# A transformer decoder in float32: its first part with three units in flight instead of two, and the loads and the gated network behind it rearranged

## The chip, the cores and the metric

One program runs on one core of a Trainium2 chip. The metric is device time in microseconds (us) of one execution. TensorE (PE; its weight loads PEld), VectorE (DVE), ScalarE (ACT) and GpSimd (POOL) run their own instruction streams in program order and wait for each other on semaphores; SyncE (SP) issues the large transfers. TensorE's results go to PSUM, eight banks of 128 x 512 float32.

## The reference

Input x is 32 sequences of 64 tokens, 128 wide, with a context of the same shape and coordinates of 3. Four layers follow; each adds to x the result of a self attention, a cross attention and a feed-forward network, each on a layer-normed x. Cut to the part that the change touches:

```python
x = x + L0_attn(ln(x), ...)          # 16 "heads" of 8, mixed over features
x = x + L0_xattn(ln(x), ctx, ...)    # softmax(q k^T / sqrt(8)) v, 16 heads
x = x + L0_ffn(ln(x), ...)           # silu(gate) * up, 384 hidden, dequantized weights
x = x + L1_attn(ln(x), ...)          # 16 heads, ternary weights
x = x + L1_xattn(ln(x), ctx, ...)    # scores of the heads mixed by a 16 x 16 matrix P
x = x + L1_ffn(ln(x), ...)           # every activation rounded to a 16 bit grid whose step
                                     # is max(abs(whole tensor)) / 32767
x = x + L2_...(x) ; x = x + L3_...(x)
```

L1_ffn needs the maximum over all 2048 tokens before it can round, four times in a row. L3's cross attention rotates queries and keys by sines and cosines of the coordinates.

## The kernel before, in words

Tokens are on partitions in 16 tiles of 128; two tiles (four sequences) make a **unit**, so there are eight. After a prologue the work has three parts with a barrier (`all_done`) between them.

**Part one** takes each unit through L0_attn, L0_xattn, L0_ffn, L1_attn, L1_xattn and the norm of L1_ffn. Two streams run side by side, each with four PSUM banks (`PS0`, `PS1`) and one arena `AR` in SBUF; four rounds make the eight units. Each engine's program is written as Python generators, one for each stream, which yield between steps; `take_turns` deals the steps out by a hand-written table `TURNS_A`, so the order on each engine is fixed in the code. On PE a third chain, `tensor_fill`, stands in the table: each step is one 128 x 128 matmul of the identity whose result nobody reads (L493). The string `FILL_A` has 471 of them.

In L0_xattn and L1_attn the 16 heads are held in four strips of 32 partitions. L745 multiplies the scores, strip r into bank r; DVE takes the maxima (L591); PE turns them over (L610); L616 computes the scores again, transposed, and L619 subtracts the maxima in the same banks; ACT takes the exponentials (L603); L641 weighs the values. In L1_xattn, L732 writes the mixed scores of a quarter of the heads into bank r, r = 0 to 3, and DVE takes the maximum (L541) and subtracts (L544).

**Part two** is L1_ffn over all tokens at once (`tensor_l1_ffn`, `scalar_l1_ffn`, `vector_l1_ffn`), in four chunks of 512 tokens. Each of its rounding steps ends in `tensor_scales` and `vector_scales`: PE turns the 128 partial maxima into a row (L1202), DVE takes its maximum, PE spreads it over partitions (L1205). Between them PE does work for part three: products of L2 weights (L1184, which need `WC`, the weights of part three), sums of gate weights (L1235, from `stat`, loaded in two halves), transposes of the sines and cosines (`tensor_angles`, L1241) and their spreading over partitions (`tensor_rotation`, L1249, a matmul of 8 rows by 512 columns), which ACT copies to `ROT` (L1305). `tensor_idle` (L1229) multiplies an identity by 512 columns into a bank that nobody reads. L1298 is the network's last product.

**Part three** is L2 and L3 in two streams.

Of the kernel before, what the change touches and what calls it, by code (L numbers as in the profile page):

```python
# [37 lines left out]
def constants():  # L38
# [22 lines left out]
    rows = np.arange(8)[:, None]  # L61
    c["sin_sel"] = np.pad(np.where(rows == d % 4, np.where(d < 4, -1.0, 1.0), 0.0), ((0, P - 8), (0, 0)))
    c["cos_sel"] = np.pad((rows - 4 == d % 4) * 1.0, ((0, P - 8), (0, 0)))
# [114 lines left out]
def decoder(nc, x, ctx_in, coords, const_d, aw_d, raw_d, intw_d, cw_d, stat_d, fd_d, out, known):  # L178
    es = ExitStack()
    with es:  # L180
# [29 lines left out]
        stream_sems = [[sem(f"{e}_stream{s}") for e in engine_names] for s in range(NS)]  # L210
        streams = [Stream(stream_sems[s], s, known) for s in range(NS)]
        SC = sb("SC", [P, NS, 640])
        for s, st in enumerate(streams):
# [12 lines left out]
            st.sc = SC[:, s, :]  # L226
        asides = [Stream(stream_sems[s], s, known, twin=st) for s, st in enumerate(streams)]
# [53 lines left out]
        S.dma_start(WC[:, :], cw_d).then_inc(wc_there, 16)  # L281

        every = [main, *streams]

        def begin(st, part, i):

            st.round = f"{part}{i}"
            tile, col = i * (NS * TS) + st.s * TS, i * (NS * ST) + st.s * ST
            st.x, st.cols = X[:, tile:tile + TS, :], slice(col, col + ST)
            st.ct = CT[:, st.cols]  # L290
# [89 lines left out]
        def pool_prologue():  # L380
            v, g = main.dve, main.pool
            for st in streams:
# [133 lines left out]
        def tensor_values(st, k, src, weight, bank):  # L516
            w4_ = weight.rearrange("p (r g n) -> p r g n", r=GR, g=2)
            for q in range(SQ):
                for g in range(2):
                    m = T.matmul(st.ps[64 * g:64 * g + 64, bank, q * SEQ:(q + 1) * SEQ],  # L520
# [3 lines left out]
        def scalar_values(st, k, bank):  # L524
            A.wait_ge(*st.pe.at(f"{k}.values"))
            for g in range(2):
                rows = slice(64 * g, 64 * g + 64)
                A.copy(st.vo[rows, :, g, :, 0:HD],
                       st.ps[rows, bank, 0:SQ * SEQ].rearrange("p (n h d) -> p n h d", h=2, d=HD)).then_inc(
                    *st.act.up(f"{k}.values{g}"))  # L530

        def vector_softmax(st, k, width, E):
            v = st.dve
            for r in range(GR):
                n = 512 // width
                sc3 = st.ps[:, r, :].rearrange("p (a k) -> p a k", k=width)
                er = E[:, 512 * r:512 * r + 512]
                mx = st.sc[:, 64 + 8 * r:64 + 8 * r + n]
                yield
                V.wait_ge(*st.pe.at(f"{k}.scores{r}"))  # L540
                V.tensor_reduce(mx, sc3, AX, ALU.max).then_inc(*v.up())  # L541
                yield
                V.wait_ge(*v.now())
                V.tensor_tensor(er.rearrange("p (a k) -> p a k", k=width), sc3, bc(mx, 2, width),  # L544
                                ALU.subtract).then_inc(*v.up(f"{k}.below{r}"))
                yield

        def scalar_softmax(st, k, parts, scale):

            def kept(u, r):
                A.wait_ge(*u.pe.at(f"{k}.turned{r}"))
                A.copy(parts(u)[1][:, 512 * r:512 * r + 512], u.ps[:, r, :]).then_inc(*u.act.up(f"{k}.turned{r}"))

            E = parts(st)[0]
            for r in range(GR):
                er = E[:, 512 * r:512 * r + 512]
                yield
                A.wait_ge(*st.dve.at(f"{k}.below{r}"))  # L560
                A.activation(er, er, ACT.Exp, scale=scale).then_inc(*st.act.up(f"{k}.exps{r}"))
                yield
                if r:
                    kept(st, r - 1)
                    yield
            kept(st, GR - 1)
            yield

        def tensor_softmax(st, k, parts, weigh, lag):


            E = parts(st)[0]
            for r in range(GR):
                yield
                T.wait_ge(*st.act.at(f"{k}.exps{r}"))
                for n in range(4):
                    m = T.transpose(st.ps[:, r, n * P:(n + 1) * P], E[:, (4 * r + n) * P:(4 * r + n + 1) * P], ident)
                m.then_inc(*st.pe.up(f"{k}.turned{r}"))
                yield
                if r >= lag:  # L580
                    weigh(st, r - lag)
                    yield
            for r in range(GR - lag, GR):
                weigh(st, r)
            yield
# [63 lines left out]
        def tensor_attention_weigh(k):  # L649
            def weigh(st, r):  # L650
                T.wait_ge(*st.act.at(f"{k}.values1"))
                T.wait_ge(*st.act.at(f"{k}.turned{r}"))
                tensor_weigh(st, k, attention_parts(st)[1], r)
            return weigh

# [25 lines left out]
        def tensor_project(st, k, weight):  # L681
            for j in range(TS):
                m = T.matmul(st.ps[:, 3, j * P:(j + 1) * P], lhsT=st.ot[:, j * P:(j + 1) * P], rhs=weight,
# [4 lines left out]
        def vector_project(st, k, scale_o, res):  # L688
            yield
            V.wait_ge(*st.pe.at(f"{k}.out"))  # L690
            V.scalar_tensor_tensor(st.x[:, :, :], st.ps[:, 3, 0:ST].rearrange("p (j d) -> p j d", d=P), scale_o, res,
# [6 lines left out]
        def tensor_attention(st, k, w, src, mix=False, rope=False):  # L698
            ps, ar = st.ps, st.ar
            E, AT = ar[:, 4096:6144], ar[:, 6144:8192]  # L700

            def keys():
                for n, wn in enumerate(("Wk", "Wkp") if rope else ("Wk",)):
# [3 lines left out]
                tensor_values(st, k, src, w(f"{k}_Wv"), 1)  # L707

# [3 lines left out]
            if own:  # L712
                yield from keys()
                yield
            for n, wn in enumerate(("Wq", "Wqp") if rope else ("Wq",)):
                m = T.matmul(ps[:, 0, n * ST:(n + 1) * ST], lhsT=w(f"{k}_{wn}"), rhs=st.xt[:, :], start=True, stop=True)
            m.then_inc(*st.pe.up(f"{k}.qk"))
            yield
            if mix:
                qp = ar[:, 0:16 * ST].rearrange("p (q g t) -> p q g t", q=SQ, g=H)  # L720
                kf = AT[:, ST:2 * ST]
                T.wait_ge(*st.act.at(f"{k}.values1"))
                for r in range(GR):
                    yield
                    T.wait_ge(*st.dve.at(f"{k}.qp{(3, 4, 11, 12)[r]}"))
                    if r in (1, 3):
                        T.wait_ge(*st.act.at(f"{k}.qp{(0, 7, 0, 15)[r]}"))
                    for q in range(SQ):
                        for g in (2 * r, 2 * r + 1):
                            o = q * P + (g % 2) * SEQ  # L730
                            for h in range(2):
                                m = T.matmul(ps[64 * h:64 * h + 64, r, o:o + SEQ], lhsT=qp[:, q, 2 * g + h, :],  # L732
                                             rhs=kf[:, q * SEQ:(q + 1) * SEQ], start=True, stop=True)
# [2015 lines left out]
```

## Time and profile before

| | |
|---|---|
| device time, median of 3 runs | 1527.18 us (1524.0 to 1532.17) |
| the profiled execution | 1525.39 us, of which its span 1524.1 us |
| part one, from 29.0 to 463.6 us of the span | 434.6 us |
| part two, to 563.1 us | 99.5 us |
| part three, to the end | 960.9 us |
| PE busy over the span | 92% |
| DVE, ACT, POOL busy | 69%, 41%, 8% |

Every fp32 matmul stands in the trace as two records, every transpose as one. Busy time of PE includes the matmuls whose results nobody reads.

### The profile page before, as it was taken

Reading aid. Unit: us, or ns where it says so; the run is one execution under the profiler, and the core shown is the slowest. Engines: PE = TensorE matmul, PEld = TensorE weight load, DVE = VectorE, ACT = ScalarE, POOL = GpSimd, SP = SyncE. Lnnn points to the kernel's source line nnn. Section 1 sums busy time; section 2 is a strip of 40 time slices with the busy share of each in tenths; the row PEclk is TensorE's granted clock in tenths of the full one; section 3 lists DMA queues with packets and bytes.
Section 4 is the critical chain, followed back from the end, with each engine's and each line's share of the span. In section 5 each row is a group of like instructions: output and inputs, shape, how many; then the busy total and the mean of one; then the engine's idle time right before and its main releaser. Section 6 shows DMA issues by size and latency. Waiting matters only on the chain.

```text
span 1524.1 us, 43988 instructions
## 1 busy us (share of the span) xinstructions
PE 1403.8 (92%) x19476; PEld 1227.7 (81%) x19476; DVE 1054.4 (69%) x2951; ACT 624.9 (41%) x1253; POOL 128.7 (8%) x267
## 2 busy tenths in 40 slices
PE   4999999999998689999988999988999988999986
PEld 3888888888884358989777998977998977998876
DVE  5758668578576958656677766678776677865666
ACT  4334344353364844532432543433543332542322
POOL 2111111111111000010000000000000000000000
PEclk9999999999999779999998999999999999999998
DMA  8000000000001110000000000000000000000001
GB/s 295 2 2 2 2 2 2 2 3 2 2 3 35 34 71 2 1 2 4 2 2 2 1 2 3 2 2 2 2 2 3 3 2 2 1 2 3 3 1 29
DMA packets 6525, 20.38 MB, mean 13 GB/s; under 512 B 2240, under 2 KB 4288, under 8 KB 5696
## 3 DMA queue, kind: packets, MB, share of 16 engines
q1 hardware_dynamic: 6336, 17.58, 3.2%
q8 instruction: 153, 2.51, 0.7%
q14 instruction: 36, 0.29, 0.1%
HBM read 16.53 MB, written 1.05 MB: 12 GB/s over the span
## 4 chain that ended last, share of the span: by engine, by line
PE 44%; DVE 13%; ACT 3%; issue 1%; POOL 1%; DVEq 0%
PE PS L2056 6%; PE PS L1917 6%; PE PS L1629 4%; PE PS L1663 4%; PE PS L1642 3%; PE PS L1674 3%; PE PS L1927 3%; DVE X L2434 2%; PE PS L1654 2%; PE PS L641 1%; PE PS L2366 1%; PE PS L493 1%; DVE AR L2427 1%; DVE mx L591 1%; PE PS L502 1%
## 5 line engine op out<-in xcount | busy, mean ns | idle before, releaser
L493 PE MATMUL PS<-CC 128*128 128x128 f32 x1460 | 204.5, 283 | 0.0
L493 PEld LDWEIGHTS PS<-CC 128*128 128x128 f32 x1460 | 185.8, 197 | 4.5 <-issue 0.5
L482 POOL TENSOR_SCALAR SC<-mv 128x2 f32<-128x2 f32 x96 | 19.7, 205 | 1223.2 <-DVE mv L470 1222.9
L2056 PE MATMUL PS<-AR,PA 64*64 64x256 f32 (+45 forms) x2624 | 112.4, 298 | 1.0 <-ACT AR L2144 0.9
L1917 PEld LDWEIGHTS PS<-AR 64*64 64x64 f32 x3072 | 103.9, 134 | 7.1 <-issue 2.5
L1917 PE MATMUL PS<-AR 64*64 64x32 f32 (+1 forms) x3072 | 107.9, 219 | 1.4 <-issue 1.0
L474 DVE TENSOR_SCALAR xn<-X,mv,SC 128x128 f32<-128x128 f32 x192 | 57.7, 343 | 56.3 <-POOL SC L485 55.7
L641 PEld LDWEIGHTS PS<-vo,AR 128*64 128x64 f32 x2560 | 81.9, 138 | 16.4 <-issue 6.6
L2056 PEld LDWEIGHTS PS<-AR,PA 64*64 64x64 f32 x2624 | 88.0, 132 | 7.2 <-issue 2.5
L641 PE MATMUL PS<-vo,AR 128*64 128x18 f32 x2560 | 88.5, 212 | 4.4 <-DVE AR L1584 2.2
L591 DVE TENSOR_REDUCE mx<-PS 128x8 f32<-128x512 f32 x96 | 60.4, 681 | 18.7 <-PE PS L745 18.7
L511 ACT COPY xt<-PS 128x256 f32<-128x256 f32 x72 | 26.9, 374 | 105.8 <-PE PS L502 105.6
L1629 PE MATMUL PS<-kvt,WC 128*128 128x128 f32 x512 | 67.9, 277 | 2.6 <-ACT kvt L1681 2.0
L485 POOL TENSOR_TENSOR SC<-SC,CC 128x2 f32<-128x2 f32 x96 | 68.7, 716 | 8.0
L1642 PE MATMUL PS<-kvt,AR 128*128 128x128 f32 x512 | 68.0, 277 | 0.9 <-ACT AR L1687 0.8
L603 ACT ACTIVATE AR<-PS 128x512 f32<-128x512 f32 x96 | 50.5, 602 | 43.0 <-PE PS L619 43.0
L1663 PE MATMUL PS<-WC,AR 128*128 128x128 f32 x512 | 67.7, 276 | 0.4 <-ACT AR L1701 0.4
L1674 PE MATMUL PS<-AR 128*128 128x256 f32 x256 | 66.2, 384 | 0.6 <-ACT AR L1698 0.5
L1642 PEld LDWEIGHTS PS<-kvt,AR 128*128 128x128 f32 x512 | 63.5, 192 | 3.7 <-ACT AR L1687 2.5
L1629 PEld LDWEIGHTS PS<-kvt,WC 128*128 128x128 f32 x512 | 62.0, 192 | 4.5 <-ACT kvt L1681 2.9
L502 PE MATMUL PS<-CC,xn 128*128 128x128 f32 x192 | 42.1, 302 | 25.4 <-DVE xn L474 23.9
L1663 PEld LDWEIGHTS PS<-WC,AR 128*128 128x128 f32 x512 | 62.4, 192 | 1.4 <-ACT AR L1701 0.9
(419 smaller groups left out, 3071.8 us busy)
## 6 DMA issues: line engine op xcount, KB each, us to landing
WC<-in_cw SPq DMA_DIRECT2D x1, 5438.5 KB, 19.1
PA<-in_fd SPq DMA_DIRECT2D x1, 2624.0 KB, 9.7
PA<-in_stat SPq DMA_DIRECT2D x2, 1280.0 KB, 6.1
CC<-in_const SPq DMA_DIRECT2D x1, 1065.0 KB, 8.2
out<-X SPq DMA_DIRECT2D x1, 1024.0 KB, 5.1
PA<-in_aw SPq DMA_DIRECT2D x1, 975.0 KB, 11.4
AR<-in_raw SPq DMA_DIRECT2D x1, 832.0 KB, 8.2
AR<-in_intw SPq DMA_DIRECT2D x1, 576.0 KB, 9.1
```

What stands on the lines that cost most here:

```text
L474: V.tensor_scalar(st.xn[:, j, :], st.x[:, j, :], st.mv[:, j, 0:1], st.sc[:, 2 + j:3 + j], ALU.subtract, ALU.mult).then_inc(*v.up(f"{k}.xn{ ...
L485: G.tensor_tensor(st.sc[:, 2:2 + TS], st.sc[:, 0:TS], cc("half_neg")[:, 0:TS], ALU.pow).then_inc(*g.up(f"{k}.rstd"))
L493: T.matmul(bank[int(b)][:, 0:P], lhsT=ident, rhs=CC[:, 0:P], start=True, stop=True)
L502: m = T.transpose(st.ps[:, 0, j * P:(j + 1) * P], st.xn[:, j, :], ident)
L591: V.tensor_reduce(st.mx[:, 32 * r:32 * r + 2 * SQ], st.ps[:, r, :].rearrange("p (a k) -> p a k", k=SEQ), AX, ALU.max).then_inc(*st.dve.up( ...
L641: m = T.matmul(out_[rows, q // 2, r, :, h, :], lhsT=AT[:, o:o + SEQ], rhs=vo[:, q, r, :, h, :], start=True, stop=True)
L1629: m = T.matmul(d.bank[:, h * P:(h + 1) * P], lhsT=G2[:, 4 * d.r + h, :], rhs=d.inputs[:, :, SEQ:KV2], start=True, stop=True)
L1642: m = T.matmul(d.bank[:, o:o + P], lhsT=d.buf[:, o:o + P], rhs=d.inputs[:, q, :], start=True, stop=True)
L1663: m = T.matmul(d.out, lhsT=d.weighed2[:, h, :], rhs=O2[:, 4 * d.r + h, :], start=(d.r == 0 and h == 0), stop=(d.r == GR - 1 and h == 3))
L1674: m = T.matmul(d.bank[:, 256 * q:256 * q + 256], lhsT=d.tokens[:, q, :], rhs=d.buf[:, 256 * q:256 * q + 256], start=True, stop=True)
L1917: m = T.matmul(ps[rows, bank, n * width:(n + 1) * width], lhsT=lhs[rows, n, :], rhs=rhs(rows, n), start=True, stop=True)
L2056: m = T.matmul(out_[:, :, first:SEQ], lhsT=FD[rows, tap:tap + 64], rhs=d.vp[rows, :, first + 1 - shift:SEQ + 1 - shift], start=starts, sto ...
```

## The change

In part one there are three streams (`trio`), each with two banks: `PS0` banks 0 and 1, `PS0` banks 2 and 3, `PS1` banks 0 and 1; the last two banks of `PS1` are free (the fills are written there or to banks not in use). Units are dealt 3, 3 and 2. The third stream's arena and tiles lie in `WC`, so `WC` is loaded at the start of part two, ahead of `stat`, and no longer in the prologue. Everything in part one that used four banks is rewritten for two: scores, maxima and exponentials of the strips go in pairs, the mixed scores through one bank, the hidden layer of L0_ffn in three pieces. All tables of turns of part one are new, and `FILL_A` has 205 letters. In part two the angles go into four strips of partitions in one step, and the rotation's matmuls are moved. Part three is the same but for its name of one attention function.

```diff
-        S.dma_start(WC[:, :], cw_d).then_inc(wc_there, 16)
+        third.s, third.ar, o = 2, WC[:, 0:ARENA], ARENA
+        for st, b in zip(trio, (PS[0][:, 0:2, :], PS[0][:, 2:4, :], PS[1][:, 0:2, :])):
+            st.ps = b
...
+        def tensor_heads(st, k, w, src):
...
+            for pair in (strips[0:2], strips[2:4]):
+                if pair[0][0]:
+                    yield
+                    T.wait_ge(*st.dve.at(f"{k}.most1"))
+                for q in range(SQ):
+                    for r, rows in pair:
+                        m = T.matmul(ps[:, r % 2, q * P:(q + 1) * P], lhsT=qm[rows, q, :, :], rhs=km[rows, q, :, :],
+                                     start=True, stop=True)
...
+            for pair in (strips[0:2], strips[2:4]):
+                if pair[0][0]:
+                    yield
+                    T.wait_ge(*st.act.at(f"{k}.exps1"))
+                for q in range(SQ):
+                    for r, rows in pair:
+                        T.matmul(ps[:, r % 2, q * P:(q + 1) * P], lhsT=km[rows, q, :, :], rhs=qm[rows, q, :, :],
+                                 start=True, stop=False)
+                    for r, rows in pair:
+                        m = T.matmul(ps[:, r % 2, q * P:(q + 1) * P], lhsT=cc("less")[rows, q * P:(q + 1) * P],
+                                     rhs=st.mt[rows, :], start=False, stop=True)
...
+        def tensor_mixed(st, k, w, src):
+            def scores(r):
+                if r == 0:
+                    T.wait_ge(*st.act.at(f"{k}.values1"))
+                else:
+                    T.wait_ge(*st.dve.at(f"{k}.below{r - 1}"))
...
+            for n in range(3):
+                if n == 2:
+                    yield
+                    T.wait_ge(*st.dve.at(f"{k}.gated0"))
+                for c in range(2):
+                    m = T.matmul(ps[:, n % 2, c * ST:(c + 1) * ST], lhsT=L0F[:, 3 * c + n, :], rhs=st.xt[:, :],
...
+        def tensor_angles():
+            for n in range(4):
+                for j in range(4):
+                    m = T.matmul(bank[0][strip(n), j * P:(j + 1) * P], lhsT=sc8[:, 4 * n + j, :], rhs=ident, start=True,
+                                 stop=True)
...
+            for n in range(4):
+                tensor_rotation(0, n)
+            tensor_rotation(1, 0)
+            tensor_rotation(1, 1)
+            for c in range(NC - 1):
+                T.wait_ge(*v.at(f"product.made{c}"))
+                tensor_idle(1, 2)
             tensor_scales("product", AM[:, 12:13])
-            tensor_idle(2, 3)
+            tensor_idle(1, 3)
...
+                if c == 0:
+                    for n in (2, 3):
+                        T.wait_ge(*a.at(f"rotation{n - 1}0"))
+                        tensor_rotation(1, n)
...
+        S.dma_start(WC[:, :], cw_d).then_inc(wc_there, 16)
         S.dma_start(stat, stat_d[:, 0:NSTAT // 2]).then_inc(stat_there, 16)
```

PE's order in the first round of part one, at the first unit's L0_xattn (745 is the scores, 610 the maxima's transpose, 616 and 619 the scores with maxima subtracted, 493 the fill; `mt` holds the transposed maxima, `xn` the normed input). Before:

```order
L745 MATMUL PS<-AR 128x128 x16
L502 MATMUL PS<-CC,xn 128x128 x2
L493 MATMUL PS<-CC 128x128 x2
L716 MATMUL PS<-xt,PA 128x256
L493 MATMUL PS<-CC 128x128 x4
L610 MATMUL PS<-CC,mx 128x128
L493 MATMUL PS<-CC 128x128
L616 MATMUL PS<-AR 128x128 x4
L619 MATMUL PS<-mt,CC 128x128 x4
```

The same place after the change (769 is the scores, 775 the transpose, 784 and 787 the subtraction; 1025 and 1032 are L0_attn of the third stream, 735 and 534 its keys and values). `PS0` holds streams one and two, `PS1` the third:

```order
L769 MATMUL PS0<-AR 128x128 x16
L1025 MATMUL PS1<-PA,WC 128x128 x4
L769 MATMUL PS0<-AR 128x128 x16
L1032 MATMUL PS1<-WC 64x128 x4
L775 MATMUL PS0<-CC,mx0 128x128
L735 MATMUL PS1<-CT,PA 128x256
L534 MATMUL PS1<-PA,CT 64x64 x8
L775 MATMUL PS0<-CC,mx1 128x128
L784 MATMUL PS0<-AR 128x128 x2
L787 MATMUL PS0<-mt0,CC 128x128 x2
```

A run of 16 scores was one unit's four strips; now it is the first two strips of two units, and the third unit's work stands where fills stood. The subtraction goes two strips at a time instead of four.

In part two, PE's order from the third `tensor_scales` on. Before (1202 and 1205 are `tensor_scales`, 1249 the rotation, 1241 the angles, 1229 the idle matmuls, 1298 the last product):

```order
L1205 MATMUL PS<-top,CC 128x1
L1249 MATMUL PS<-AR,CC 128x512 x4
L1241 MATMUL PS<-CC,PA 8x128 x8
L1249 MATMUL PS<-AR,CC 128x512 x4
L1229 MATMUL PS<-CC 128x512 x4
L1202 MATMUL PS<-CC,AM 1x128
L1205 MATMUL PS<-top,CC 128x1
L1229 MATMUL PS<-CC 128x512 x3
L1298 MATMUL PS<-PA,AR 128x128 x48
```

After (1346 and 1349 are `tensor_scales`, 1396 the rotation, 1373 the idle matmuls, 1446 the last product):

```order
L1349 MATMUL PS1<-top,CC 128x1
L1396 MATMUL PS0<-AR,CC 128x512
L1396 MATMUL PS1<-AR,CC 128x512 x3
L1396 MATMUL PS0<-AR,CC 128x512 x2
L1373 MATMUL PS0<-CC 128x512 x6
L1346 MATMUL PS1<-CC,AM 1x128
L1349 MATMUL PS1<-top,CC 128x1
L1373 MATMUL PS0<-CC 128x512 x3
L1446 MATMUL PS0<-PA,AR 128x128 x12
L1396 MATMUL PS1<-AR,CC 128x512 x2
L1446 MATMUL PS0<-PA,AR 128x128 x36
```

Six rotations stand ahead of `tensor_scales` instead of eight with the angles between, and two stand inside the last product.

## Rows read from the trace of the kernel before

**Rows 1.** The page: busy time of the engines.

```profile
PE 1403.8 (92%) x19476; PEld 1227.7 (81%) x19476; DVE 1054.4 (69%) x2951; ACT 624.9 (41%) x1253; POOL 128.7 (8%) x267
```

**Rows 2.** Windows: length, PE, PEld, DVE, ACT, POOL busy (records), clock, DMA, GB/s.

```profile
29.00:463.60 434.60, 416.04 (x6334) 360.04 (x6334) 296.04 (x840) 179.98 (x393) 59.58 (x120) 0.99 0.02 5
463.60:563.10 99.50, 79.08 (x315) 43.56 (x315) 73.97 (x93) 63.23 (x75) 3.71 (x3) 0.83 0.08 27
563.10:1524.00 960.90, 899.23 (x12782) 816.41 (x12782) 668.36 (x1944) 365.69 (x751) 57.63 (x128) 0.98 0.02 6
...
200.00:300.00 100.00, 96.51 (x1520) 83.50 (x1517) 70.30 (x204) 41.80 (x92) 14.17 (x29) 1.00 0.01 2
```

**Rows 3.** Timeline of part one: start, length, engine, line, operation, tiles, records.

```profile
37.50 5.52 PE L493 MATMUL PS<-CC 128*128 128x128 f32 x48
...
58.59 1.17 PE L745 MATMUL PS<-AR 32*128 32x128 f32 x32
59.69 0.44 PE L502 MATMUL PS<-CC,xn 128*128 128x128 f32 x2
...
63.52 0.40 PE L616 MATMUL PS<-AR 32*128 32x128 f32 x8
63.74 0.40 PE L619 MATMUL PS<-mt,CC 32*128 32x128 f32 x8
```

**Rows 4.** Groups by line and shape, 30 to 448 us: busy, mean ns, idle before.

```profile
L591 DVE TENSOR_REDUCE mx<-PS 128x8 f32<-128x512 f32 x64 | 40.1, 681 | 16.5 <-PE PS L745 16.5
...
L603 ACT ACTIVATE AR<-PS 128x512 f32<-128x512 f32 x64 | 33.8, 602 | 27.6 <-PE PS L619 27.6
...
L1044 DVE SCALAR_TENSOR_TENSOR AR<-AR,PS 128x768 f32<-128x768 f32 x8 | 7.6, 952 | 17.3 <-ACT AR L1033 17.3
...
L1050 DVE TENSOR_TENSOR X<-X,PS 128x256 f32<-128x256 f32 x8 | 3.4, 420 | 3.2 <-PE PS L1023 3.2
```

**Rows 5.** Timeline: the mixed scores of one unit.

```profile
435.42 3.95 PE L732 MATMUL PS<-AR 128*64 128x64 f32 x128
```

**Rows 6.** Timeline of part two, up to the gated network's second rounding.

```profile
463.62 0.33 SPq L1495 DMA_DIRECT2D PA<-in_stat  x1
...
492.40 2.06 PE L1184 MATMUL PS<-WC 64*128 64x128 f32 x32
...
494.39 1.04 PE L1241 MATMUL PS<-CC,PA 128*8 128x128 f32 x8
...
495.26 4.48 PE L1235 MATMUL PS<-PA,CC 128*80 128x256 f32 x20
...
512.85 0.37 ACT L1352 COPY G1S<-PS 80x256 f32<-80x256 f32 x1 [0.29 <-PE PS L1235]
...
513.12 1.49 ACT L1322 ACTIVATE AR<-AR 128x1536 f32<-128x1536 f32 x1
...
516.25 0.95 DVE L1418 TENSOR_SCALAR AR<-AR 128x1536 f32<-128x1536 f32 x1
```

**Rows 7.** Transfers: size, median us from issue to landing.

```profile
WC<-in_cw SPq DMA_DIRECT2D x1, 5438.5 KB, 19.1
...
PA<-in_stat SPq DMA_DIRECT2D x2, 1280.0 KB, 6.1
```

**Rows 8.** Timeline of part two, its last rounding and last product.

```profile
534.24 7.16 PE L1249 MATMUL PS<-AR,CC 8*128 8x512 f32 x8 [2.06 <-ACT AR L1309]
...
539.82 0.16 DVE L1441 TENSOR_REDUCE AM<-AM 128x1 f32<-128x4 f32 x1
...
541.33 5.57 PE L1229 MATMUL PS<-CC 128*128 128x512 f32 x8
...
547.04 0.28 DVE L1212 TENSOR_REDUCE top<-PS 1x1 f32<-1x128 f32 x1 [7.07 <-PE PS L1202]
...
550.43 11.32 PE L1298 MATMUL PS<-PA,AR 128*128 128x128 f32 x96
```

**Rows 9.** A window of 5 us in part two, columns as in rows 2.

```profile
535.00:540.00 5.00, 5.00 (x7) 1.99 (x6) 4.73 (x4) 1.14 (x1) 0.00 (x0) 0.50 0.02 3
```

More of the change, by code:

```diff
@@ L528, in scalar_values @@
                 A.copy(st.vo[rows, :, g, :, 0:HD],
-                       st.ps[rows, bank, 0:SQ * SEQ].rearrange("p (n h d) -> p n h d", h=2, d=HD)).then_inc(
+                       st.ps[rows, bank, o:o + SQ * SEQ].rearrange("p (n h d) -> p n h d", h=2, d=HD)).then_inc(
                     *st.act.up(f"{k}.values{g}"))
[L532 to L585, printed above, removed]
@@ L707, in keys @@
                 tensor_values(st, k, src, w(f"{k}_Wv"), 1)
+            yield from tensor_norm(st, k, early=(keys,))
+            T.wait_ge(*st.act.at(f"{k}.xt"))
+            for n, wn in enumerate(("Wq", "Wqp")):
+                m = T.matmul(ps[:, 0, n * ST:(n + 1) * ST], lhsT=w(f"{k}_{wn}"), rhs=st.xt[:, :], start=True, stop=True)
+            m.then_inc(*st.pe.up(f"{k}.qk"))
+            yield
+            qm = ar[:, 0:2 * ST].rearrange("p (q h t) -> p q h t", q=SQ, h=2)
+            km = ar[:, 2 * ST:4 * ST].rearrange("p (q h t) -> p q h t", q=SQ, h=2)
@@ new lines, in tensor_rope_attention @@
+            T.wait_ge(*st.act.at(f"{k}.operands"))
+            T.wait_ge(*st.dve.at(f"{k}.operands"))
+            for q in range(SQ):
+                for r in range(GR):
+                    rows = slice(32 * r, 32 * r + 32)
+                    m = T.matmul(ps[:, r, q * P:(q + 1) * P], lhsT=qm[rows, q, :, :], rhs=km[rows, q, :, :],
+                                 start=True, stop=True)
+                    if q == SQ - 1:
+                        m.then_inc(*st.pe.up(f"{k}.scores{r}"))
+            yield
@@ L709, in tensor_attention, with tensor_keys, tensor_queries, keys @@
+        def tensor_keys(st, k, w, src):
+            T.matmul(st.ps[:, 1, 0:ST], lhsT=w(f"{k}_Wk"), rhs=src[:, :], start=True, stop=True)
+            tensor_values(st, k, src, w(f"{k}_Wv"), 1, ST)
+        def tensor_queries(st, k, w, src):
+            def keys():
+                tensor_keys(st, k, w, src)
+                yield
             own = src is st.xt
@@ new lines, in vector_mixed @@
+        def vector_mixed(st, k, w, mix):
+            ps, v, (E, AT), (qp, qf, kf) = st.ps, st.dve, attention_parts(st), mixing(st)
+            yield from vector_norm(st, k)
+            V.wait_ge(*st.pe.at(f"{k}.qk"))
+            V.tensor_scalar(qf, ps[:, 0, 0:ST], w(f"{k}_bq"), None, ALU.add).then_inc(*v.up(f"{k}.qf"))
+            yield
+            V.wait_ge(*v.now())
+            for g in range(H):
+                if g % 8 < 5:
+                    V.tensor_scalar(qp[:, :, g, :], qf.rearrange("p (q t) -> p q t", q=SQ), mix[:, g:g + 1], None,
+                                    ALU.mult).then_inc(*v.up(f"{k}.qp{g}"))
+                if g == 8:
+                    yield
+            yield
+            sc3 = ps[:, 0, :].rearrange("p (a k) -> p a k", k=SEQ)
+            for r in range(GR):
+                er = E[:, 512 * r:512 * r + 512].rearrange("p (a k) -> p a k", k=SEQ)
+                mx = st.sc[:, 64 + 8 * r:72 + 8 * r]
+                V.wait_ge(*st.pe.at(f"{k}.scores{r}"))
+                V.tensor_reduce(mx, sc3, AX, ALU.max).then_inc(*v.up())
@@ L1100, in pool_part_a @@
         def pool_part_a(st):
-            for i in range(NITER):
+            for i in range(units(st)):
                 begin(st, "a", i)
@@ L1159, in decoder @@
             fill = [tensor_fill(FILL_A)] if engine == "tensor" else []
-            take_turns([part(st) for st in streams] + fill, TURNS_A[engine])
+            take_turns([part(st) for st in trio] + fill, TURNS_A[engine])
         all_done()
+        for st, b in zip(streams, PS):
+            st.ps = b
         U = flat[:, 0:6144].rearrange("p (k n) -> p k n", k=3)
```

534 lines of the change are left out of this document (308 added, 226 removed), and 77 rows, old and new, of the table TURNS_A.

## The prediction

> **What bounds the kernel now.** I read the page first, then the windows of the three parts, then the timeline inside two of them. PE is busy for 92% of the span, DVE for 69%, ACT for 41% [rows 1]. The windows show where that holds: part one has PE busy for 416.0 of 434.6 us and DVE for 296.0; part two is looser, 79.1 of 99.5 us; part three has PE at 899 of 961 us [rows 2]. Part three's code and tables stay, so I give it nothing (its rows would have to move by over 5 us to matter).
>
> A PE busy for 96% looks like a PE bound part, but the source says otherwise: 471 of its 3311 matmuls in part one are fills that nobody reads. A run of 48 records, that is 24 fills, takes 5.52 us [rows 3], so one is 0.23 us and all of them 108 us, a quarter of the part. What really sets a round of two units (434.6 / 4 = 108.7 us) is the chain of steps inside a unit, with real PE work of only about 77 us in it (416 - 108 over four). So there is room for a third unit, and the question is what the two-bank form costs.
>
> **Part one, PE's work.** PE executes its order whatever comes, so I count it.
>
> Removed: 471 - 205 = 266 fills at 0.23 us = -61.2 us.
>
> Unchanged in number: all other matmuls (2840 before and after, by the order).
>
> Dearer: the strip matmuls. L616 and L619 each issue four matmuls (eight records) on four strips, and the next four start 0.22 us later [rows 3]. One strip alone has two records of 128 columns in that time, 0.11 us each, which is the same as a record of the fill (5.52 / 48 = 0.115). So a strip runs at its full rate and the gain came from four of them side by side: 0.056 us a matmul. With pairs, two strips run side by side and the same 0.22 us gives two matmuls, 0.112 each. There are 768 of them (three kinds, 16 for each of two attentions, eight units): 768 x 0.056 = +43.0 us. This is the change's largest cost and nothing hides it, since it is PE's own time. The bounds: 0 if the other strips found work (nothing stands between the pairs in the order but the same pairs), and 43 as taken.
>
> Switches: a block of 16 strip matmuls should take 0.90 us at that rate, and the next kind starts after 1.10 [rows 3], so entering or leaving strips costs 0.2 us. Runs of strips go from 27 to 46 in the order: +3.8 us. Runs of all kinds go from 458 to 413, so the others fall by 64; at 0.1 each (between nothing and that 0.2) -6.4 us. Net -2.6.
>
> The Trainium skill (TensorEngine Tiling (Array Packing), Key Properties) says that changing the tiling mode drains the engine, a rule against this change, as it cuts strips into more pieces. The row agrees with a cost but prices it at 0.2 us, so by the rule the sum only bears the 3.8 us already in it.
>
> Busy PE after: 416.0 - 61.2 + 43.0 - 2.6 = 395.2 us.
>
> **Part one, idle PE.** Before: 434.6 - 416.0 = 18.6 us [rows 2], start and end included. Can the rest keep up? DVE: the same work, but L0_ffn's two products of 768 columns at 0.95 us become six of 256, at 0.42 us like L1050 [rows 4]: 8 x (2.5 - 1.9) = +5, so 301 us in 416, 72%. ACT gains three shorter activations for one, some 3 us on 180. POOL is at 60. The unit's own chain grows, because banks are shared. Heads: scores wait for the first two maxima (+1.2 us: two of 0.68 [rows 4] less overlap) and the second subtraction for the first two exponentials (two of 0.60 [rows 4] and a second block of 0.9, together +2.1), twice a unit: +6.6. Mixed scores: 3.95 us a unit [rows 5], 1.0 us a quarter; each now waits until DVE has drained the one bank (1.4 us) and DVE waits for it, +4. L0_ffn +1. So a chain of 108.7 becomes about 120 us. Three units' real PE work is (395.2 - 205 x 0.23) / 8 x 3 = 131 us: PE becomes the bound while three are in flight (two rounds), the chain in the last round with two units. 2 x 131 + 120 = 382 us, plus the start and what fills cannot cover, stays below the PE sum; both views agree that idle need not grow much. In the stretches with three units the order has hardly a fill, so a late input is no longer absorbed. I take 21 us of idle, between 5 (all but start and end gone) and 45.
>
> Part one: 395.2 + 21 = 416.2 us, against 434.6: **-18.4 us**.
>
> **Part two.** WC is issued where stat was, 463.6, and first needed by L1184 at 492.4, 28.8 us later; it took 19.1 us to land, and stat behind it 6.1, so 25.2 against the 31.6 until L1235 [rows 6, 7]. Cost 0, hidden by the hidden layer's 48 matmul records; if the load took 30 us instead, each us over comes onto PE but DVE and ACT would lose only that. POOL's 3.7 us of products then start 20 us later, and nothing but the barrier waits.
>
> The angles: 8 transposes were 8 records in 1.04 us; 16 plain matmuls are 32 records, some 3.6 us, so PE reaches the gate sums 2.6 us later and the second half of stat with them. ACT already waited 0.29 us for that sum at 512.85, and its next tanh (513.12, 1.49 us) feeds DVE at 516.25 [rows 6]: 1.6 us of slack. 2.6 - 1.6 = +1.0 us.
>
> The last rounding: the maximum is there at 539.98, but PE is still in rotations and idle matmuls at half clock (0.50 [rows 9]) until 546.9, and DVE waits 7.07 us [rows 8]. After the change the rotations use four strips side by side (4 of them in about 1.7 us at that clock, where 7.16 us were four in one strip), and the idle matmuls hang on the products' arrival, so PE is free: 7.07 less a handoff of 0.5 = -6.6 us. Two rotations inside the last product: +1.0 us (512 columns, two strips abreast, and two switches). ACT puts gated_scaled(3) ahead of the copies: -0.2.
>
> Part two: **-4.8 us**. Bounds: 0 to -7 at full clock. The clock is the risk: the last product (11.3 us [rows 8]) ran at full clock (96 records, 0.118 each, as the fills) after PE had been busy without a pause for over 10 us (534.2 to 546.9). The idle matmuls may not do that now; then up to 11 us come back.
>
> The prologue: 0 (no engine there waits for WC's 5.4 MB; bounds 0 to -1). Sum: -18.4 - 4.8 = **-23.2 us**. Against the profiled execution (span 1524.1, with 1.3 around it: 1525.4) that is 1502.2; the median of the runs lies 1.8 higher, so 1527.2 - 23.2 = **1504 us**.
>
> **The rivals.**
> - *Waits eat it* (no change). With three units and no fills, PE's 43.5 us a unit and DVE's 37.6 are both near 87% of a round of 131, each in a fixed order. If idle grows from 21 to 41 us, about 1524. For it: a wait on either engine now holds up two other units. Against: before, PE lost only 3.5 us in 100 in the middle of the part [rows 2]. 0.14.
> - *The chain sets the pace* (slower). A unit with two banks takes 120 us beside one other; beside two it queues on every engine. It decides at (434.6 - 120) / 2 = 157 us a round; at 165 the part takes 450, total about 1538. Against: it needs 34 us of waiting a round over the 131 that PE works. 0.08.
> - *The clock falls in part two's end.* +11 us: about 1515, still faster. 0.09.
> - *Strips don't cost double*: 43 us less, about 1461. Only the rows' rate of one strip speaks against it, and firmly. 0.03.
> - My forecast: 0.66, by itself 1491 to 1515 (idle 5 to 30).
>
> 0.5% of this kernel, 7.6 us, is about what a measurement can tell from no change. Faster: 0.66 + 0.09 + 0.03 = 0.78; same 0.14; slower 0.08. For 8 in 10 the range takes the forecast, the clock and part of the first rival: 1487 to 1520.
>
> **What the profile after would show.** Part one near 416 us with PE busy 395; L784 and L787 in groups of four records every 0.22 us (0.11 would refute the cost of pairs); DVE busy about 301. The third stream's last norm two thirds through. In part two, L1328 without a wait for WC; DVE's wait for the last row of maxima under 1 us; clock near 1 at the last product. The prediction is wrong if PE's idle in part one leaves 5 to 45 us, or if the chain of waits shows PE waiting mostly on DVE's maxima (L541's successor) while three units are in flight.

## The result

Before, 1529.8 us (median of 20 runs, 1521.3 to 1542.3); after the change, 1523.3 us (20 runs, 1499.6 to 1534.6). The ratio taken first, 0.986 (95% interval 0.983 to 0.990), leaves out the ten longest runs of the changed kernel, those with the lowest mean clocks (0.949 to 0.955), and with them a part of what the change does to the clock. The medians of all 20 runs differ by only 6.5 us, a ratio of 0.996. On two later occasions, with every run counted, the same kernel gave 0.990 (0.985 to 0.995) and 0.994 (0.991 to 0.997), its medians 13.8 and 10.0 us under those of the kernel before. So the change is worth 0.4 to 1.4%, and 0.4 to 1.0% where every run counts. The prediction, 1504 from 1527.2, was a ratio of 0.985: the first ratio agrees, the others say that 9 to 17 of its 23 us did not arrive.

The page of the changed kernel, to set beside [rows 1]:

```profile
span 1526.6 us, 43026 instructions
...
PE 1408.2 (92%) x18964; PEld 1233.5 (81%) x18964; DVE 1055.0 (69%) x2983; ACT 628.2 (41%) x1269; POOL 130.7 (9%) x271
...
PEclk9999999999999699989999999799999899999999
```

The mean clock of this execution is 0.953. A second execution of the same kernel (span 1509.1 us, mean clock 0.971) is read with it. Windows of the three parts, columns as in [rows 2], first in the first execution:

```profile
29.00:447.95 418.95, 402.84 (x5802) 347.07 (x5802) 295.69 (x872) 182.81 (x409) 60.11 (x120) 0.97 0.01 2
447.95:548.10 100.15, 78.77 (x335) 45.40 (x335) 73.62 (x93) 63.83 (x76) 4.10 (x3) 0.81 0.21 82
548.10:1526.00 977.90, 917.41 (x12782) 833.52 (x12782) 669.57 (x1944) 365.56 (x751) 57.61 (x128) 0.96 0.02 6
```

and in the second:

```profile
29.00:442.50 413.50, 396.28 (x5802) 340.74 (x5803) 295.73 (x872) 182.76 (x410) 60.12 (x120) 1.00 0.01 2
442.50:540.10 97.60, 76.39 (x335) 44.14 (x335) 74.09 (x93) 63.81 (x75) 3.91 (x3) 0.84 0.21 84
540.10:1509.00 968.90, 906.94 (x12782) 824.04 (x12782) 669.51 (x1944) 365.56 (x751) 57.61 (x128) 0.97 0.02 6
```

Against [rows 2], part one is 21.1 us shorter in the second execution, where its clock is 1.00, and part two 1.9 us; part three, whose code was not touched, is 8.0 us longer there and 17.0 in the first. One profile of part one says little to a few us: in the eight profiles that have the new part one with all its fills it took 412.6 to 419.1 us, 15.6 to 22.0 less than the 434.6 before. DVE's and ACT's busy time in part three is the same to 1.2 us; only PE's grew, with the clock at 0.97 and 0.96 where it was 0.98.

The strips of part one, in the timeline of the second execution (tiles in `WC` are the third stream's, those in `AR` of the other two):

```profile
92.66 0.49 PE L784 MATMUL PS<-WC 32*128 32x128 f32 x4
92.99 0.39 PE L787 MATMUL PS<-WC,CC 32*128 32x128 f32 x4
93.21 0.39 PE L784 MATMUL PS<-WC 32*128 32x128 f32 x4
93.43 0.39 PE L787 MATMUL PS<-WC,CC 32*128 32x128 f32 x4
...
107.17 1.16 PE L769 MATMUL PS<-AR 32*128 32x128 f32 x16
108.25 1.99 PE L1149 MATMUL PS<-WC,PA 128*128 128x256 f32 x8
```

Four records every 0.22 us where [rows 3] has eight; and half a block of scores (16 records) keeps the next kind away for 1.08 us, as long as the whole block of 32 did.

### The profile page after: what moved, and what is told of

The parts are those of the page before. It is cut to its first block, busy times and chain, and to the rows that moved or that the text cites. A ratio compares the mean times of both kernels' runs of the same rounds, so it can differ in the third digit from the quotient of the medians.

```text
span 1526.6 us, 43026 instructions
## 1 busy us (share of the span) xinstructions
PE 1408.2 (92%) x18964; PEld 1233.5 (81%) x18964; DVE 1055.0 (69%) x2983; ACT 628.2 (41%) x1269; POOL 130.7 (9%) x271
## 4 chain that ended last, share of the span: by engine, by line
PE 46%; DVE 12%; ACT 3%; POOL 1%; issue 1%; DVEq 0%; ACTq 0%
PE PS L2069 7%; PE PS L2208 6%; PE PS L1781 4%; PE PS L1815 4%; PE PS L1794 3%; PE PS L1826 3%; PE PS L2079 3%; DVE X L2586 2%; PE PS L1806 2%; PE PS L507 2%; PE PS L600 1%; PE PS L2518 1%; DVE AR L2579 1%; POOL SC L499 1%; DVE mx L550 1%
## 5 line engine op out<-in xcount | busy, mean ns | idle before, releaser
L507 PE MATMUL PS<-CC 128*128 128x128 f32 x928 | 137.2, 291 | 0.0
L507 PEld LDWEIGHTS PS<-CC 128*128 128x128 f32 x928 | 123.3, 203 | 3.8 <-issue 0.5
L2208 PE MATMUL PS<-AR,PA 64*64 64x256 f32 (+44 forms) x2624 | 117.5, 308 | 0.7 <-ACT AR L2296 0.7
L2069 PEld LDWEIGHTS PS<-AR 64*64 64x64 f32 x3072 | 112.2, 144 | 6.5 <-issue 2.7
L600 PEld LDWEIGHTS PS<-vo,AR 128*64 128x64 f32 x2176 | 69.2, 140 | 12.1 <-issue 6.6
L600 PE MATMUL PS<-vo,AR 128*64 128x18 f32 x2176 | 73.9, 214 | 3.6 <-DVE AR L1736 2.1
L2301 ACT ACTIVATE AR<-AR,CC 128x256 f32<-128x256 f32 x64 | 29.1, 502 | 86.4 <-DVE AR L2406 61.7
L499 POOL TENSOR_TENSOR SC<-SC,CC 128x2 f32<-128x2 f32 x84 | 60.3, 718 | 6.9
L1853 ACT COPY AR<-PS 128x512 f32<-128x512 f32 x64 | 37.3, 584 | 51.3 <-PE PS L1826 51.1
L1843 ACT ACTIVATE AR<-AR 128x512 f32<-128x512 f32 x64 | 40.4, 631 | 41.6 <-DVE AR L1869 41.5
## 6 DMA issues: line engine op xcount, KB each, us to landing
WC<-in_cw SPq DMA_DIRECT2D x1, 5438.5 KB, 15.6
```

What stands on the lines that cost most here:

```text
L499: G.tensor_tensor(st.sc[:, 2:2 + TS], st.sc[:, 0:TS], cc("half_neg")[:, 0:TS], ALU.pow).then_inc(*g.up(f"{k}.rstd"))
L507: T.matmul(bank[int(b)][:, 0:P], lhsT=ident, rhs=CC[:, 0:P], start=True, stop=True)
L600: m = T.matmul(out_[rows, q // 2, r, :, h, :], lhsT=AT[:, o:o + SEQ], rhs=vo[:, q, r, :, h, :], start=True, stop=True)
L1843: A.activation(d.buf, d.buf, ACT.Exp, scale=D2 ** -0.5).then_inc(*st.act.up(f"{d.name}.exps"))
L2069: m = T.matmul(ps[rows, bank, n * width:(n + 1) * width], lhsT=lhs[rows, n, :], rhs=rhs(rows, n), start=True, stop=True)
L2208: m = T.matmul(out_[:, :, first:SEQ], lhsT=FD[rows, tap:tap + 64], rhs=d.vp[rows, :, first + 1 - shift:SEQ + 1 - shift], start=starts, sto ...
```

## The experiments

**The changed kernel again**, for a second profile and interval.

> The changed kernel once more, for its time beside the others of this group and for a second profile. Theory: part one about 416 us with PE busy near 397, part two 95 to 100 us, part three 961 us where TensorE's clock stays up, ratio to before 0.985. Rival: part three is longer than before by some 10 us in this profile too, although its code is the same, so something of part one or two is handed on to it; then the clock would not differ in part three while its length does.

Measured: 1521.3 us (6 runs), ratio 0.990 (0.985 to 0.995). Its rows are above. Part three was longer, as the rival has it, but not at the same clock, which the rival asks for: the clock is lower, 0.97.

**Pairs of strips in the kernel before**: nothing but the order of part one's strip matmuls.

```diff
-            for q in range(SQ):
-                for r, rows in strips:
+            for pair in (strips[0:2], strips[2:4]):
+                for q in range(SQ):
+                    for r, rows in pair:
```

> The kernel before, with one thing changed in part one: the matmuls on strips of L0_xattn and L1_attn go in pairs of strips (first 0 and 1, then 2 and 3) into the same four banks; fills, streams, tables stay. Theory (a strip runs at its own full rate, 0.11 us a record, and only strips side by side save time): 768 matmuls dearer by 0.056 us, PE busy in part one 416 + 43 = 459 us, part one about 470 to 478 us, kernel +36 to +43 us, ratio 1.024 to 1.028. Rival (the rate is one of issue, 0.028 us a record whatever the strips): no change, ratio 1.00.

Measured: 1557.5 us, ratio 1.015 (1.009 to 1.022). Part one:

```profile
29.00:487.90 458.90, 442.54 (x6334) 389.92 (x6334) 296.47 (x840) 181.38 (x393) 59.60 (x120) 0.99 0.02 5
```

PE busy grew by 26.5 us, not 43. To see why, I added up, over all of PE's rows of part one's timeline, the time from each row's start to the next row's start, waits left out:

```
us of PE in part one            before   pairs in before   after
fills (L493, L507)               125.4        122.6         54.8
three kinds of strip matmuls      48.9         78.7         95.3
all others                       241.3        240.9        246.0
```

The pairs alone cost 29.8 us: where the second pair follows the first at once, the border between them overlaps (a block of scores went from 1.10 to 1.65 us, not to 2.16, twice the 1.08 of a half that stands alone). In the changed kernel other work of 128 rows stands between the pairs, and the strips cost 46.4 us. So 43.0 was nearly right for the changed kernel, and its account was not: 29.8 us are two strips abreast instead of four, 16.6 us the blocks cut apart. The Trainium skill (TensorEngine Tiling (Array Packing), Key Properties) says that changing the tiling mode drains the engine. The traces agree that more pieces cost time, 16.6 us for the blocks of 16 attentions; how much of that is a drain, and how much the lost overlap of the two pairs, they do not tell apart.

**No fills in part one.** The changed kernel without its 205 fills there.

```diff
-        FILL_A = ("5555666...
+        FILL_A = ""
```

> The changed kernel without any fill in part one (part three's stay). 205 fills are 47 us of PE's time. Theory (with three units in flight the fills stand nearly all where PE would wait anyway): part one 0 to 8 us shorter, PE idle in it about 21 + 40 us, with the granted clock lower in its first 25 us and in its last round; kernel -5 us, ratio to the changed kernel 0.995 to 1.00. Rival (the fills delay real work): part one 20 us shorter or more. Second rival (without fills the clock falls often): part one 5 us or more longer, granted clock of part one under 0.93.

Measured: 1574.4 us, ratio 1.025 (1.020 to 1.030). Part one:

```profile
29.00:499.70 470.70, 411.74 (x5392) 345.29 (x5393) 297.75 (x872) 183.11 (x409) 60.10 (x120) 0.82 0.01 2
```

54.8 us of fills are gone and PE is busy for 15.5 us more, at a mean clock of 0.82 instead of 1.00; idle time went from 17.2 to 59.0. That is the second rival. The fills are not only cover for waits; they hold the clock.

**Only the early fills, and half of the late ones.** First the 54 fills before 100 us alone (the edit below), then these and every other one of the 151 later (`if i < 54 or i % 2`, which keeps 75 of them and leaves out 76). Both edits went through a function that part three also calls, so that 205 and 103 of part three's fills are missing as well, which was not meant: only part one is read.

```diff
             for i, b in enumerate(banks):
+                if i < 54:
                     T.matmul(bank[int(b)][:, 0:P], lhsT=ident, rhs=CC[:, 0:P], start=True, stop=True)
```

> The changed kernel with only the first 54 of part one's 205 fills (all before 100 us); 151 are left out. If fills only take time: 40 us of TensorE work less, waits grow by some 15 to 25, part one 390 to 400 us. If the later fills hold the clock: the profile without any fill had done the same number of records by 109 us as the one with all, so the whole loss lies later; part one 460 to 475 us, granted clock 0.82 to 0.88 there, ratio to before 1.015 to 1.025.

> The changed kernel with the first 54 fills and every other one of the 151 after them (75 left out). If fills only take time: part one 400 to 405 us. If the clock depends on them step by step: half the loss of the kernel without fills, 435 to 445 us. If half of them is enough for the clock: 395 to 410 us with the granted clock at 0.98 or more, and this is the best kernel.

Measured: 1608.0 us (median of four runs, 1580.5 to 1610.8; its profile is of the shortest, and there is no ratio) and 1527.0 us, ratio 0.998 (0.994 to 1.001). Part one of the first:

```profile
29.00:482.40 453.40, 405.80 (x5501) 342.83 (x5501) 296.97 (x873) 183.19 (x409) 60.13 (x120) 0.86 0.01 2
```

and of the second:

```profile
29.00:458.80 429.80, 398.86 (x5650) 340.07 (x5651) 296.40 (x872) 183.30 (x410) 60.11 (x120) 0.95 0.01 2
```

No theory's length of part one was hit (only the clock of 0.86 lies where the second theory of the first kernel had it), but the order is plain: 205, 129, 54 and no fills give a clock of 1.00, 0.95, 0.86 and 0.82 and a part one of 413.5, 429.8, 453.4 and 470.7 us. The last 76 fills, 20 us of work at 0.27 each, save 16 us against the profile of 413.5, and 11 against the longest of the eight (419.1); the other two steps, 24 and 17 us, are larger than that spread of 6.4. The early 54 save 17 as well, against my expectation, which took them for free because the same number of records was done by 109 us.

**The new part two alone**, in the kernel before.

> The kernel before with the change's part two alone: angles in four strips, rotations moved, idle matmuls tied to the products; the weights of part three stay in the prologue, part one is that of before. Theory: the wait for the last row of maxima goes from 7.1 to 0.5 us, the angles cost 1 us, the rotations inside the last product 1 us: part two 99.5 - 4.8 = 94.7 us at full clock. Rival (seen in the profile of the changed kernel): the clock is at half when the three idle matmuls before the last product run, and gives 2.5 us back: part two 97 to 98 us. Kernel -2 to -5 us, ratio 0.997 to 0.999.

Measured: 1530.4 us, ratio 0.997 (0.994 to 1.000); part two 99.2 us in its profile, 1.2 of that from four records of idle matmuls at its start, 3.17 us where the kernel before had 1.96, at the lower clock. Less that 1.2 it is 98.0, where the rival has it, and its cause is there too: the three idle matmuls ahead of the last product took 5.49 us. Part three took 955.1 us.

**The new part one alone**: the changed kernel with the old network.

> The changed kernel with the old network of part two (angles in two steps, rotations in one strip each), so only the three units in flight and the load of WC behind part one are new. If the two halves of the change add up: part one 413 to 419 us as in the changed kernel, part two 99.5 to 101 us, sum 18 to 21 us less than before in a profile. If the longer third part (969 and 978 us in two profiles of the changed kernel, 955 to 962 in three with the old part one; its length less the time lost to the clock is 941 to 944 in all) comes with the new part one: part three 965 to 978 us here with 25 to 37 us lost, and a ratio of 0.990 to 0.995. If that was chance: part three 955 to 962 and a ratio near 0.987.

Measured: 1518.0 us, ratio 0.991 (0.988 to 0.994).

```profile
29.00:441.75 412.75, 396.30 (x5802) 340.71 (x5802) 295.78 (x872) 182.92 (x409) 60.14 (x120) 0.99 0.01 2
441.75:540.90 99.15, 79.15 (x315) 44.13 (x315) 73.75 (x93) 63.27 (x75) 3.90 (x3) 0.83 0.21 83
540.90:1505.00 964.10, 902.40 (x12782) 818.53 (x12782) 669.05 (x1944) 365.89 (x751) 57.65 (x128) 0.98 0.02 6
```

The gain is part one's. Part three lies just under the 965 of the one theory and just over the 962 of the other; the ratio lies in the first one's range (0.990 to 0.995).

**No idle matmuls ahead of the last product.**

```diff
             tensor_scales("product", AM[:, 12:13])
-            tensor_idle(1, 3)
```

> The changed kernel without the three idle matmuls between the product's scale and the last product. In the profile of the changed kernel those three took 5.49 us at half the clock and the last product began 2.6 us after its first rows were there; it then ran 12 us at nearly full clock. Theory one (the idle matmuls only stand in the way): the last product starts 2.6 us earlier and part two is about 2.5 us shorter than 97.6. Theory two (their work is what brings the clock up): the product's first 48 records run at half the clock, 5 to 6 us are lost on them, and part two is 100 to 103 us.

Measured: 1516.7 us, ratio 0.989 (0.985 to 0.992). The end of part two:

```profile
527.98 0.37 PE L1346 MATMUL PS<-CC,AM 128*1 128x128 f32 x1 [3.44 <-DVE AM L1591]
528.73 0.58 PE L1349 MATMUL PS<-top,CC 1*128 1x1 f32 x2 [0.37 <-DVE top L1356]
532.08 5.46 PE L1445 MATMUL PS<-PA,AR 128*128 128x128 f32 x24 [2.77 <-DVE AR L1601]
537.47 1.30 PE L1396 MATMUL PS<-AR,CC 8*128 8x512 f32 x4
538.70 8.30 PE L1445 MATMUL PS<-PA,AR 128*128 128x128 f32 x72
```

and in the changed kernel (second execution):

```profile
519.89 0.37 PE L1346 MATMUL PS<-CC,AM 128*1 128x128 f32 x1 [3.44 <-DVE AM L1592]
520.63 0.58 PE L1349 MATMUL PS<-top,CC 1*128 1x1 f32 x2 [0.37 <-DVE top L1356]
521.14 5.49 PE L1373 MATMUL PS<-CC 128*128 128x512 f32 x6
526.43 2.94 PE L1446 MATMUL PS<-PA,AR 128*128 128x128 f32 x24
529.29 1.13 PE L1396 MATMUL PS<-AR,CC 8*128 8x512 f32 x4
530.35 8.30 PE L1446 MATMUL PS<-PA,AR 128*128 128x128 f32 x72
```

From L1346 on, the product starts after 4.1 us instead of 6.5, and its first 24 records then take 5.46 instead of 2.94. The last record ends 19.0 against 18.8 us after L1346. Each theory holds in its first half, and the two effects cancel: the start comes 2.4 us earlier, and 24 records, not the 48 forecast, run at half the clock, which costs 2.5 us and not 5 to 6. Part two took 100.4 us in this profile, and 97.5, 97.6 and 100.2 in the three of the changed kernel.

**Idle matmuls in the pause, angles behind the first sums.**

```diff
             for c in range(NC - 1):
                 T.wait_ge(*v.at(f"product.made{c}"))
-                tensor_idle(1, 2)
+                tensor_idle(1, 5 if c == NC - 2 else 2)
...
-            tensor_angles()
             tensor_gate_sums(0)
+            tensor_angles()
```

> The changed kernel with two edits in part two: five idle matmuls in place of two behind the third quarter of the product, and the angles behind the first half of the gate sums instead of ahead of it. In the changed kernel TensorE paused 3.44 us ahead of the last maximum and then ran at half the clock until 526.4. If the pause causes that, the granted clock in the last 20 us of part two is 1.00, the three idle matmuls take 2.9 instead of 5.5 us and the last product begins 2.5 us earlier. If the angles cause VectorE's wait of 1.08 us for the tanh (they put off the second half of stat by 2.9 us), that wait falls to 0.1. Both: part two 94.0 to 94.5 us against 97.6. If neither holds: 97 to 98.

Measured: 1505.2 us, ratio 0.986 (0.981 to 0.992). Part two took 93.5 us; its window, and PE's rows at its end:

```profile
442.40:535.90 93.50, 74.50 (x341) 43.24 (x341) 74.01 (x93) 63.57 (x75) 3.90 (x3) 0.89 0.22 88
...
513.10 4.56 PE L1373 MATMUL PS<-CC 128*128 128x512 f32 x10 [1.47 <-DVE AR L1588]
518.53 0.27 PE L1346 MATMUL PS<-CC,AM 128*1 128x128 f32 x1 [0.87 <-DVE AM L1592]
519.17 0.38 PE L1349 MATMUL PS<-top,CC 1*128 1x1 f32 x2 [0.37 <-DVE top L1356]
519.48 2.84 PE L1373 MATMUL PS<-CC 128*128 128x512 f32 x6
522.32 2.92 PE L1446 MATMUL PS<-PA,AR 128*128 128x128 f32 x24
```

The pause ahead of L1346 fell from 3.44 to 0.87 us, the clock stayed at 1.00, and the end comes 16.0 us after L1346 instead of 18.8. VectorE's wait for the tanh, 1.08 us in the changed kernel, is gone from its timeline, as the second theory of the expectation has it. Two other profiles name its cause: with the new angles and the weights in the prologue (the new part two alone) the wait is 1.18 us, and with the old angles and the weights loaded in part two (the new part one alone) there is none. So it is the angles and not the load.

**That kernel and the changed one side by side, and a pause ahead of part three.**

> The changed kernel with five idle matmuls behind the third quarter and the angles behind the first gate sums, once more, beside the changed kernel itself on the same chip. Part two 93.5 us as before. If the shorter part two is kept: 4 us (0.3%) under the changed kernel. If the 16 us between the two medians of the earlier runs were real and not the clock: ratio 0.980 to 0.985.

> The changed kernel again, beside its variants. Part one 413 to 419 us, part two 97.6 to 100.4, part three 965 to 978; ratio to before 0.986 to 0.990.

> The changed kernel with 12 more maxima on VectorE (1.75 us each, 21 us) behind part two, in which TensorE has nothing to do; their results go nowhere. If TensorE's load just before part three is what costs the clock there: part three loses 10 to 18 us instead of 25 to 37 and takes 953 to 961, and the kernel is 10 us slower than the changed one instead of 21. If it does not matter: part three 965 to 978, the kernel 21 us slower (ratio 1.000 to 1.005).

```diff
         vector_l1_ffn()
+        for _ in range(12):
+            V.wait_ge(*main.dve.now())
+            vector_most(0, chunk(Gt, 0))
         all_done()
```

Measured: 1509.7 us, ratio 0.988 (0.984 to 0.992), for the mended kernel; 1522.6 us, 0.994 (0.991 to 0.997), for the changed one; 1530.4 us, 1.000 (0.998 to 1.003), with the pause. Parts two and three of the kernel with the pause, and then of the changed kernel beside it:

```profile
444.58:565.81 121.23, 78.81 (x335) 45.35 (x335) 94.65 (x105) 63.85 (x75) 4.01 (x3) 0.77 0.17 68
565.81:1526.00 960.19, 898.67 (x12782) 816.84 (x12782) 668.70 (x1944) 365.96 (x751) 57.86 (x128) 0.98 0.02 6
...
441.63:539.13 97.50, 76.51 (x335) 44.29 (x335) 74.15 (x93) 63.85 (x75) 3.90 (x3) 0.84 0.21 84
539.13:1507.00 967.87, 905.82 (x12782) 822.53 (x12782) 669.51 (x1944) 365.86 (x751) 57.63 (x128) 0.97 0.02 6
```

By the medians (10 and 12 runs), 21 us of work that nobody needs cost only 7.8 us over the changed kernel, so some 13 us came back. The two profiles show where 7.7 of them did, in part three (960.2 against 967.9 us); they themselves lie 18.9 us apart, with 23.7 more in part two and 3.0 more in part one. The first theory holds for the length of part three and nearly for the time; the loss to the clock there, 19.1 us in the table below, is just over its 10 to 18.

## Why part three became longer

Of every profile I took windows of 5 us over part three and added up what the clock took, the sum of (1 - clock) x 5 us over windows with a clock under 0.95:

```
part three                            length  lost to the clock  difference
before                                 960.9        17.9           943.0
new part two alone                     955.1        11.0           944.1
pairs in before                        961.7        20.7           941.0
new part one alone                     964.1        21.6           942.5
pause ahead of part three              960.2        19.1           941.1
no fills in part one                   964.8        20.6           944.2
mended part two, two profiles   966.1, 962.8  24.7, 20.0   941.4, 942.8
no last idle matmuls                   971.6        31.2           940.4
changed kernel, three profiles  977.9, 968.9, 967.9  37.5, 26.5, 24.8  940.4, 942.4, 943.1
```

The windows are whole ones; the last piece of each part, under 5 us, is left out, and with it the losses are up to 2.3 us larger. The last column is the same for all twelve profiles within 4 us (within 6 with the last pieces), where the lengths differ by 23, so the clock explains nearly all of part three's difference.

The runs without a profile say the same of the whole kernel. An estimate of what each run lost is its span times (1 - its mean clock), which also counts idle time. Its median is 47.4 us in the kernel before (29 runs), 56.1 with the new part one alone (12), 61.5 in the changed kernel (12 runs, the third occasion) and 50.5 in the one with part two mended (6). Less that loss, the span's median is 1457.6 us in the changed kernel and 1483.4 in the kernel before. So by this estimate the change is worth some 25 us at an equal clock, close to the 23 forecast; the clock takes 14 of them back, and 10 were measured.

The clock falls in part three while PE is fully busy. The last of these rows is from the kernel before, at the same place as the second (130 us into part three); the others are from the changed kernel's first execution:

```profile
668.10:678.10 10.00, 10.00 (x125) 8.86 (x126) 4.04 (x13) 4.01 (x10) 0.00 (x0) 0.98 0.01 2
678.10:688.10 10.00, 10.00 (x184) 9.53 (x185) 6.02 (x21) 1.80 (x4) 0.00 (x0) 0.50 0.01 3
958.10:968.10 10.00, 10.00 (x97) 9.47 (x96) 6.88 (x13) 1.98 (x4) 0.00 (x0) 0.50 0.01 2
...
693.10:703.10 10.00, 10.00 (x360) 9.69 (x357) 7.29 (x24) 1.98 (x4) 0.00 (x0) 1.00 0.02 5
```

No wait precedes the fall at 678.1. The kernel before runs the same matmuls there (most are of 64 rows by 64 columns) and finishes 360 records in 10 us instead of 184. Such stretches, 130, 410 and 650 us into part three and 3 to 17 us long, stand in all three profiles of the changed kernel and in that without its last idle matmuls; the kernel before, the new part one alone and the kernel with the pause have none at these places. The last of them differs from the changed kernel in nothing but the 21 us in which PE rests ahead of part three, and its profile and its median together say that the rest helps. It is not the only thing that does: the kernel with part two mended has no such rest, and neither of its two profiles has the stretches at 130 and 410 us. And the one at 130 is not found in the changed kernel alone: without fills in part one it is there too (13.7 us, and none at 410 and 650), and the kernel before with pairs has a short one (3.4 us). So the loss grows with the change, over many runs, but what sets it off at these places stays open. That they lie where PE works on small matmuls may be part of it; no run tests that.

## Why the prediction came out as it did

- **Part one, -18.4 us; measured -21.1** (-15.6 to -22.0 over the eight profiles). The mechanism is the one forecast: fills give way to a third unit's work, and strips cost double. PE busy was forecast at 395.2 and is 396.3, and that it agrees to 1.1 us is luck, since the terms are off by more and cancel. Fills: forecast -61.2, measured -70.6, since a fill costs 0.27 on average in both kernels, with its changes of kind, not the 0.23 of a long run. Strips: +43.0 against +46.4, by the two causes above and not the one forecast. Switches and the rest: -2.6 against +4.7. Idle: 21 against 17.2. DVE stayed at 295.7 where I had 301.
- **Waits, chain.** Idle time fell, so *waits eat it* and *the chain sets the pace* are both out; three units kept PE busy 396 of 413.5 us. PE's longest waits in part one are for the normed input (7.2 us, 6.8 of them at once) and not for DVE's maxima. *Strips don't cost double* is out by the 46.4.
- **WC, 0: right.** It landed 15.6 us after its issue and L1328 began 0.31 us behind L1349, with no wait.
- **The angles, +1.0: right,** by the way forecast, and **DVE's wait for the product's maxima, -6.6: right.** Both stand in DVE's timeline of the changed kernel (second execution), the one as a wait of 1.08 us for the tanh, the other as 0.47 us where [rows 8] has 7.07:

```profile
496.36 0.96 DVE L1569 TENSOR_SCALAR AR<-AR 128x1536 f32<-128x1536 f32 x1 [1.08 <-ACT AR L1474]
...
519.67 0.16 DVE L1592 TENSOR_REDUCE AM<-AM 128x1 f32<-128x4 f32 x1
520.30 0.28 DVE L1356 TENSOR_REDUCE top<-PS 1x1 f32<-1x128 f32 x1 [0.47 <-PE PS L1346]
```

- **The last product: mis-sized.** Forecast +1.0 for the rotations less 0.2. From the last L1202 on [rows 8] it took 15.0 us (546.74 to 561.75), after the change 18.8. The rotations are 1.1 of the 3.8; the rest is the three idle matmuls at half the clock (5.49 us, 2.8 at the full one), behind a pause of PE of 3.44 us that the new order opens and the old one did not have. I had named this risk with up to 11 us and left it out of the sum. With -6.6 for DVE's wait, +1.1 for the angles and +3.8 for the last product part two is -1.7; measured -1.9, forecast -4.8.
- **Part three, 0: the step that failed.** I gave it nothing because its code stays. Its code does, its clock does not: +7 to +17 us in the changed kernel's profiles. It is most of why the medians of all runs (1521 to 1523) lie over my 1504 and just over the 1520 of my range, and why two of the three ratios (0.990 and 0.994) lie nearer to no change than my 0.985. The kernel before also ran somewhat longer beside them, 1530 to 1535 us where I had 1527. The rows of before could have warned me only in part: its own part three has the clock at 0.98.

## What to carry to other kernels

Price a matmul that nobody reads by what it does to the clock too: here 76 fills, 20 us of work, saved 11 to 16 us net. Narrow tiles lose twice when a unit gets fewer banks, once by fewer strips abreast and once by the blocks cut apart; keep what is left of them in one piece. A part that isn't touched still needs its clock compared, and its length less what the clock took is the number to compare between two profiles.

The version to keep is the changed one with five idle matmuls in the pause and the angles moved: 1505.2 and 1509.7 us, 27.2 and 22.9 under the kernel before beside it, and 12.8 under the changed kernel beside it. Part two accounts for 4 of the 12.8, in both of its profiles. The others go with the clock: the estimate of what the runs lost to it is 11 us lower, part two's share included. The two intervals (0.984 to 0.992, 0.991 to 0.997) still overlap, so more than those 4 us is likely and not shown.

## What the runs showed of the hardware

The granted clock of a busy core went to 0.50 for 10 us and longer with PE busy all that time, in part three of each profile of the changed kernel (10 to 17 us from 410 us into it). The Trainium skill (TensorE: Matmul & The Clock Gate, Part 1) says that the slow state is the default of an idle engine and that activity releases it. Part one without fills agrees (0.82 against 1.00); the window from 678.1 to 688.1 us does not, and there the measurement decides: the engine was busy without a gap and ran at the lower of its two levels, 1.2 GHz. Two pairs of strips that follow each other overlap at their border, which is worth 0.5 us a block (1.65 us for 32 records of scores, where two separate halves take 1.08 each; 16.6 us over 32 such blocks).
